# Early tiles of self-attention: normalising and turning spread over six middle rounds of a cross-attention loop

## What is computed

```python
x = x + _L0_xattn_ref(_layernorm(x), ctx_768, ...)   # 16 heads of 16, keys and values from the context
x = x + _L0_attn_ref(_layernorm(x), ...)             # rmsnorm * norm_w, q/k/v projections, causal attention
x = x + _L0_ffn_ref(...); x = x + _L1_xattn_ref(...); x = x + _L1_attn_ref(...); x = x + _L1_ffn_ref(...)
```

## Time and profile before

| | us |
|---|---|
| three runs | 1916.33, 1922.88, 1923.32 |
| median | 1922.88 |
| profiled execution | 1919.42 |
| its span, first to last instruction | 1917.6 |

### The profile page before, as it was taken

One profiled execution on the slowest core, in us unless ns is written; L12 is line 12 of the kernel. 1 busy time (PEld: TensorE's weight loads), 2 busy tenths in 40 slices (PEclk: granted clock), 3 DMA queues, 4 the chain that ended last, 5 costly groups with the idle time before them and its releaser, 6 DMA issues.

```text
span 1917.6 us, 44031 instructions
## 1 busy us (share of the span) xinstructions
PE 1819.1 (95%) x17698; PEld 1540.1 (80%) x17698; DVE 1275.4 (67%) x2718; ACT 940.7 (49%) x2038; POOL 912.3 (48%) x1133
## 2 busy tenths in 40 slices
PE   5999999999999789999999999999999999899998
PEld 4788888888888667879999999999999976656665
DVE  5788888888888765656666767666666745752222
ACT  4666666666666534453444444444444434522221
POOL 4677777777777427337433333343333213513232
PEclk9999999999999897999999999999999999999999
DMA  5112111211111010042223222222233006051110
GB/s 158 37 44 64 37 37 37 60 48 36 37 36 51 9 46 1 2 113 80 81 76 85 61 61 61 61 61 61 65 86 92 1 29 261 1 187 30 24 32 13
DMA packets 50424, 113.06 MB, mean 59 GB/s; under 512 B 4864, under 2 KB 36944, under 8 KB 48688
## 3 DMA queue, kind: packets, MB, share of 16 engines
q1 hardware_dynamic: 45808, 105.13, 18.5%
q0 software_dynamic: 4416, 5.12, 1.5%
HBM read 105.78 MB, written 5.37 MB: 58 GB/s over the span
## 4 chain that ended last, share of the span: by engine, by line
PE 77%; DVE 9%; ACT 7%; issue 3%; DMA 2%; POOL 0%; SPq 0%; POOLq 0%; DVEq 0%; ACTq 0%
PE ps L164 8%; PE ps L104 7%; PE ps L2578 6%; PE ps L495 5%; PE ps L476 5%; PE ps L1642 4%; PE ps L453 4%; PE ps L2602 3%; PE ps L470 3%; PE ps L1643 2%; DVE arena L1754 2%; PE ps L404 2%; DVE arenaR L1748 2%; PE ps L1629 2%; PE ps L1628 2%
## 5 line engine op out<-in xcount | busy, mean ns | idle before, releaser
L562 DVE TENSOR_REDUCE arena<-ps 128x1 f32<-128x400 f32 (+1 forms) x512 | 257.6, 565 | 92.3 <-PE ps L453 92.2
L700 ACT ACTIVATE arena<-ps 128x384 f32<-128x384 f32 (+1 forms) x512 | 223.5, 525 | 103.5 <-PE ps L476 103.5
L777 POOL TENSOR_TENSOR arena<-arena 128x512 f32<-128x512 f32 (+1 forms) x157 | 204.7, 1304 | 92.6 <-ACT arena L700 82.9
L1642 PE MATMUL ps<-arenaR 128*128 128x386 f32 x768 | 242.9, 374 | 1.1 <-DVE arenaR L1748 1.1
L1858 ACT CAST arenaR<-ps 128x512 fp32r<-128x512 f32 (+1 forms) x256 | 116.6, 508 | 202.2 <-PE ps L164 201.4
L1643 PE MATMUL ps<-arenaR 128*128 128x194 f32 x768 | 194.3, 253 | 0.0
L1748 DVE TENSOR_TENSOR arenaR<-ps,arenaR 128x512 fp32r<-128x512 f32 (+1 forms) x256 | 138.9, 585 | 28.6 <-ACT arenaR L1858 28.6
L1643 PEld LDWEIGHTS ps<-arenaR 128*128 128x128 f32 x768 | 147.5, 192 | 0.0
L1642 PEld LDWEIGHTS ps<-arenaR 128*128 128x128 f32 x768 | 145.5, 189 | 1.4 <-DVE arenaR L1748 1.4
L1883 ACT ACTIVATE wsb<-ps,arena 128x1200 f32<-128x1200 f32 x64 | 80.9, 1264 | 131.6 <-DVE arena L1807 131.6
L1754 DVE TENSOR_REDUCE arena<-ps 128x1 f32<-128x400 f32 (+1 forms) x256 | 137.2, 566 | 1.5 <-PE ps L1632 1.4
(11 more groups left out here) (372 smaller groups left out, 4806.8 us busy)
## 6 DMA issues: line engine op xcount, KB each, us to landing
wsb<-in_ctx SPq DMA_DIRECT2D x16, 1152.0 KB
arena<-in_ctxT SPq DMA_DIRECT2D x16, 800.5 KB, 5.2
arena<-in_ctxT SPq DMA_DIRECT2D x32, 400.2 KB, 7.3
wsb<-in_ctxT SPq DMA_DIRECT2D x16, 800.5 KB, 5.1
wsb<-in_ctxT SPq DMA_DIRECT2D x32, 400.2 KB, 7.4
gu<-in_m_gu SPq DMA_DIRECT2D x8, 1536.0 KB, 18.0
dn<-in_m_dn SPq DMA_DIRECT2D x8, 768.0 KB, 10.3
wsb<-in_f_w SPq DMA_DIRECT2D x2, 1024.0 KB, 6.1
```

What stands on the lines that cost most here:

```text
L562: e.tensor_reduce(mx4[n % 2][:, u, i:i + 1], ps[:, at("look", n, i, u), 0:400 + (i == 3)], AX.X, ALU.max).then_inc(c.maxed.at((n, i, u)), 1)
L700: e.activation(v[:, u, 0:128 * GN[s]], ps[:, at("st", n, s, u), 0:128 * GN[s]], ACT.Exp).then_inc(c.exp_a.at((x0, n, s, u)), 1)
L777: e.tensor_tensor(acc_p[0:k], acc_p[0:k], v[0:k, :, 128 * t:128 * t + 128], ALU.add).then_inc(added_p.at((n, s)), 1)
L1642: e.matmul(o, PTh[:, t, :], v[:, t, 0:386], start=(t == 0), stop=False)
```

## The change

Tiles 0 to 5 (`SA_EARLY = 6`) are normalised one by one at the end of DVE's rounds 51 to 56 and turned one by one at the end of PE's rounds 52 to 57, both halves of a tile in one bank. ACT alone copies them out of PSUM, with `norm_w`, into the plain transposed buffer `hT` (`take_h`, two copies of 128 x 128), in its same round; the buffer is free since the last queries of the first stage. In round 60 ACT copies all six tiles (1536 columns) from `hT` to the high part, and in round 61 DVE subtracts to get the low part; both read SBUF. POOL's roots move to round 50 and cover six tiles. Tiles 6 and 7 are normalised, turned (four transposes) and taken between the projections; ACT takes the high part after its share of tile 0's projection instead of tile 1's, DVE the low part ahead of tile 1's sum of squares instead of behind it. The gammas move to round 0. Of the weight copies on ACT one stays at the end of round 59, one moves into round 60 behind the first exponentials, one to the end of round 61, one stays in 63; the weight subtractions on DVE are in rounds 59, 60, 62 and 63. For the last pair the two accumulators lie in the buffers of the weights `wk` and `wv`, which are no longer read, so its first additions wait for no totals.

```diff
-    acc_d, acc_p = ar(128, 4, 128), ar(128, 4, 128)
+    sums_d, sums_p = ar(128, 4, 128), ar(128, 4, 128)
+    def acc(n):
+        if n < N - 1:
+            return sums_d, sums_p
+        return [flat(W[k]).rearrange("p (u c) -> p u c", c=128) for k in ("wk", "wv")]
...
             if s == 0:
-                if n:
-                    w.wait_ge(*(added_p((n - 1, "all")) if n < N - 1 else totals(n - 1)))
+                if n == N - 1:
+                    w.wait_ge(*w_lo("wk"))
+                elif n:
+                    w.wait_ge(*added_p((n - 1, "all")))
...
             if s == 0:
-                if n:
+                if 1 <= n < N - 1:
                     w.wait_ge(*totals(n - 1))
...
             for use in groups(r)[:1]:
                 exps(*use)
+            then.act(e, w, r, 0, at)
...
-            then.act(e, w, r, at)
+            then.act(e, w, r, 1, at)
...
-SA_PARTS = ((0, 1, 2, 3), (4, 5, 6), (7,))
+SA_EARLY = 6
...
-    return [(r - 60, k) for k in range(2)] if r in (60, 61) else []
+    return r - 52 if 0 <= r - 52 < SA_EARLY else None
...
+    def turn_pe(e, w, t, bank):
+        w.wait_ge(*c.normed((sa, t)))
+        for k in range(2):
+            p = c.turn(e, ps[:, bank, 128 * k:128 * k + 128], c.h[:, t, 128 * k:128 * k + 128])
+        p.then_inc(c.hT_turned.at((sa, t)), 1)
+
+    def turn_last_pe(e, w, k):
+        w.wait_ge(*c.normed((sa, NT - 1)))
+        for i in range(2):
+            p = c.turn(e, ps[:, k, 128 * i:128 * i + 128], c.h[:, SA_EARLY + i, 128 * k:128 * k + 128])
+        p.then_inc(c.hT_turned.at((sa, "last", k)), 1)
...
-    def dve_ahead(e, w, r, at):
-        if r == 59:
+    def dve_ahead(e, w, r):
+        if r == 0:
...
-            for t in SA_PARTS[0]:
-                norm_tile_rms(e, w, t)
-        if r == 60:
-            for t in SA_PARTS[1]:
-                norm_tile_rms(e, w, t)
-        if 60 <= r <= 63:
-            split_low(e, w, r - 60)
-        for part, k in sa_turns(r):
-            take_low(e, w, part, k, at("sa", part, k))
+        if 0 <= r - 51 < SA_EARLY:
+            norm_tile_rms(e, w, r - 51)
+        if r in (59, 60, 62, 63):
+            split_low(e, w, (59, 60, 62, 63).index(r))
+        if r == 61:
+            u = slice(0, 128 * SA_EARLY)
+            w.wait_ge(*c.hT_act((sa, "high")))
+            e.tensor_tensor(hTl[:, :, u], hT[:, :, u], hTh[:, :, u], ALU.subtract).then_inc(c.hT_dve.at((sa, "early")), 1)
...
             if t == 0:
+                norm_tile_rms(e, w, SA_EARLY)
                 norm_tile_rms(e, w, NT - 1)
...
-            squares(t)
             if t == 1:
                 for k in range(2):
-                    take_low(e, w, 2, k, k)
+                    take_low(e, w, k)
+            squares(t)
...
+    def take_h(e, w, t, bank):
+        w.wait_ge(*c.hT_turned((sa, t)))
+        w.wait_ge(*c.q_made(("x0", NT - 1)))
+        w.wait_ge(*c.in_const("small"))
+        w.wait_ge(*c.po("zeros"))
+        for k in range(2):
+            p = e.activation(hT[:, k, 128 * t:128 * t + 128], ps[:, bank, 128 * k:128 * k + 128], ACT.Identity, bias=c.zeros[:, 0:1],
+                             scale=c.normw[:, k:k + 1])
+            p.then_inc(c.hT_act.at((sa, t) if k else None), 1)
...
-        for i in {59: (0, 1), 60: (2,), 63: (3,)}.get(r, ()):
+        for i in {(59, 1): (0,), (60, 0): (1,), (61, 1): (2,), (63, 1): (3,)}.get((r, place), ()):
             split_high(e, w, i)
-        for part, k in sa_turns(r):
-            take_high(e, w, part, k, at("sa", part, k))
+        if place and sa_turns(r) is not None:
+            take_h(e, w, sa_turns(r), at("sa", sa_turns(r)))
+        if (r, place) == (60, 1):
+            u = slice(0, 128 * SA_EARLY)
+            w.wait_ge(*c.hT_act((sa, SA_EARLY - 1)))
+            ctx_done(w)
+            e.copy(hTh[:, :, u], hT[:, :, u]).then_inc(c.hT_act.at((sa, "high")), 1)
...
             project(t)
-            if t == 1:
+            if t == 0:
                 for k in range(2):
-                    take_high(e, w, 2, k, k)
+                    take_high(e, w, k)
...
-        u = slice(NT - 1, NT) if last else slice(0, NT - 1)
+        u = slice(SA_EARLY, NT) if last else slice(0, SA_EARLY)
...
     def pool_ahead(e, w, r):
-        if r == 58:
+        if r == 50:
             root_rms(e, w, False)
```

More of the change, by code:

```diff
@@ L337, in latents @@
             at("o", projects(r))
-        for part, k in then.turns(r):
-            at("sa", part, k)
+        if then.turns(r) is not None:
+            at("sa", then.turns(r))
         if r == 2 * N - 2:
@@ L500, in values @@
                 w.wait_ge(*padded("rows"))
+                acc_d, acc_p = acc(n)
                 for u in range(4):
@@ L542, in pe @@
                 project(projects(r))
-            for part, k in then.turns(r):
-                bk = take("sa", part, k)
-                then.turn_pe(e, w, part, k, bk)
-                emptied[bk] = c.hT_dve(("sa", part, k))
+            if then.turns(r) is not None:
+                bk = take("sa", then.turns(r))
+                then.turn_pe(e, w, then.turns(r), bk)
+                emptied[bk] = c.hT_act(("sa", then.turns(r)))
     def dve(e, w):
@@ L649, in dve @@
                 invert(r // 2 - 1)
-            then.dve(e, w, r, at)
+            then.dve(e, w, r)
         gather(N - 1)
@@ L766, in add @@
         def add(n, s):
-            v = probs(n, s)
+            v, acc_p = probs(n, s), acc(n)[1]
             w.wait_ge(*c.exp_a((x0, n, s, 3)))
             if s == 0:
-                if n:
+                if 1 <= n < N - 1:
                     w.wait_ge(*totals(n - 1))
@@ L781, in add_both @@
             w.wait_ge(*added_p((n, 3)))
-            e.tensor_tensor(acc_p, acc_p, acc_d, ALU.add).then_inc(added_p.at((n, "all")), 1)
+            e.tensor_tensor(sums_p, sums_p, sums_d, ALU.add).then_inc(added_p.at((n, "all")), 1)
         def scale(n):
@@ L840, in latents @@
     return pe, dve, act, pool, sp, ended, raw_done, ctx_done
-SA_PARTS = ((0, 1, 2, 3), (4, 5, 6), (7,))
+SA_EARLY = 6
 def sa_turns(r):
-    return [(r - 60, k) for k in range(2)] if r in (60, 61) else []
+    return r - 52 if 0 <= r - 52 < SA_EARLY else None
 def selfattn(c, m, ahead, ctx_done, ended, then):
-    d, ps, psf = c.d, c.ps, c.psf
+    d, ps, psf, hT = c.d, c.ps, c.psf, c.hT
     parts = Carve(m.sap)
@@ L897, in sp @@
         e.dma_start(caus, d["causal"]).then_inc(in_caus.at("in", 16), 16)
-    def part_of(t):
-        return 0 if t < 4 else 1 if t < NT - 1 else 2
-    def columns(part):
-        return slice(128 * SA_PARTS[part][0], 128 * SA_PARTS[part][-1] + 128)
-    def turned(part, bank):
-        return ps[:, bank, 0:128 * len(SA_PARTS[part])]
     def project_pe(e, w, t, which, emptied):
@@ L913, in project_pe @@
             o = slice(512 * (i % 2), 512 * (i % 2) + 512)
-            w.wait_ge(*c.hT_dve((sa, part_of(t), 1)))
+            w.wait_ge(*c.hT_dve((sa, "early") if t < SA_EARLY else (sa, 1)))
             w.wait_ge(*w_lo(i))
@@ L922, in project_pe @@
         return p
-    def turn_pe(e, w, part, k, bank):
-        w.wait_ge(*c.normed((sa, SA_PARTS[part][-1])))
-        o = turned(part, bank)
-        for i, t in enumerate(SA_PARTS[part]):
-            p = c.turn(e, o[:, 128 * i:128 * i + 128], c.h[:, t, 128 * k:128 * k + 128])
-        p.then_inc(c.hT_turned.at((sa, part, k)), 1)
+    def turn_pe(e, w, t, bank):
[8 more added lines that the diff above has]
+        p.then_inc(c.hT_turned.at((sa, "last", k)), 1)
     def pe_ahead(e, w, emptied):
@@ L1010, in pe @@
             w.wait_ge(*emptied[k])
-            turn_pe(e, w, 2, k, k)
-            emptied[k] = c.hT_dve((sa, 2, k))
+            turn_last_pe(e, w, k)
+            emptied[k] = c.hT_dve((sa, k))
         project(2, (2, 3, 0, 1))
@@ L1036, in norm_tile_rms, with take_low @@
     def norm_tile_rms(e, w, t):
-        w.wait_ge(*c.po(("rooted", sa, t == NT - 1)))
+        w.wait_ge(*c.po(("rooted", sa, t >= SA_EARLY)))
         e.tensor_scalar(c.h[:, t, :], c.x[:, t, :], c.mv[:, t, 0:1], c.rs[:, t:t + 1],
                         ALU.subtract, ALU.mult).then_inc(c.normed.at((sa, t)), 1)
-    def take_low(e, w, part, k, bank):
-        u = columns(part)
-        w.wait_ge(*c.hT_act((sa, part, k)))
-        w.wait_ge(*c.in_const("small"))
-        e.scalar_tensor_tensor(hTl[:, k, u], turned(part, bank), c.normw[:, k:k + 1], hTh[:, k, u], ALU.mult,
-                               ALU.subtract).then_inc(c.hT_dve.at((sa, part, k)), 1)
+    def take_low(e, w, k):
+        u = slice(128 * SA_EARLY, 1024)
+        w.wait_ge(*c.hT_act((sa, "last", k)))
+        e.scalar_tensor_tensor(hTl[:, k, u], ps[:, k, 0:256], c.normw[:, k:k + 1], hTh[:, k, u], ALU.mult,
+                               ALU.subtract).then_inc(c.hT_dve.at((sa, k)), 1)
     def split_low(e, w, i):
```

13 lines of the change are left out of this document (6 added, 7 removed).

## The result

The changed kernel took 1905.65 us (median of 10 runs, 1899.91 to 1913.18) against 1918.96 us (10 runs, 1912.12 to 1925.27) of the kernel before: 0.9933 times, 95% interval 0.9912 to 0.9955. By that ratio it is 12.9 us less (13.3 by the two medians).

The account below looks back on a forecast made before the run. The prediction took TensorE (PE), busy 95% of the span, as the bound, with losses where it waits or runs at low clock. +2.7 - 15.2 - 2.2 - 2.2 = -16.9 us from a mean of 1920.5 gave 1904 us, range 1898 to 1914.

Parts of the forecast that it names:

- Middle rounds: Rounds 51 to 57: two added PE transposes in each of six rounds cost 0.45 us a round, +2.7 us; ends 1.6 and 5.
- gap plus shift are 1.03 us, so the pair is covered: Middle rounds: ScalarE's two new copies, about 0.8 us, fit its 0.58 us gap plus PE's 0.45 us later scores.
- a rest of 0.3 would delay maxima: Middle rounds: DVE's added normalisation is hidden for 1.1 of 1.35 us; the rest delays only maxima whose banks PE needs next round.
- Rounds 59 to 64: Last cross-attention rounds: without L1046's waits and with early last-head additions, the first projection starts 16.0 us earlier, taken as 15.2.
- in this chain no wait of PE is over 1.5 us: Rounds 61 and 62: PE runs from scores to totals, ending near 659.5, with no wait above 1.5 us.
- 0.8 us for operations of DVE and POOL that fall on each other: Last rounds: allowance for DVE and POOL additions colliding, reducing the 16.0 us gain to 15.2.
- second rival: Last rounds: the adders bind, DVE's order keeps its old pace, gain 9 us instead of 15.2, 1910 us; chance 0.13.
- The twelve matmuls: First projections: matmuls now at the low clock, 0.43 us each, would run at 0.23, saving some 11 x 0.20 = 2.2 us.
- first rival: From 655 us on the clock stays low, giving back 4.4 us and the twelve matmuls' 2.2 us, 1910 us; chance 0.15.
- The wait for L1046 in the projections: Projections: PE's 2.5 us wait for DVE's low part goes, less 0.27 us for two more transposes, net 2.2 us.
- The third rival: Nothing comes of it: another bank or POOL's additions replace L1046, only the 2.5 us wait goes, 1920 us; chance 0.06.
- the fourth: Rival: turnings stall PE in rounds 52 to 57 and the clock falls there, making it slower, up to 1955 us; chance 0.04.

Follow-up runs that it names:

- e7: Changed kernel with each early tile turned and copied ahead of the round's value products on PE and ScalarE; 1905.14 us in one execution, rounds 51 to 57 71.81 us.
- e5: Changed kernel with tile 0's normalisation moved behind the queries' copy in DVE's round 52; 1901.75 us in one execution, rounds 51 to 57 71.59 us.
- e4: Changed kernel with the last head's sums back in the common place, waiting for the totals before; 1907.67 us, 0.9934 of the kernel before.
- e9: Changed kernel with POOL's additions for head 30's last two groups cut to a quarter width; round 59 to the first projection 38.58 us against 40.0.
- e6: Changed kernel with DVE's last three weight subtractions moved to rounds 62, 63 and 64; 1911.11 us in one execution, round 59 to projection 38.90 us.
- e3: Kernel before with only the last head's sums in their own place; 1918.97 us, 0.9989 of the kernel before.
- e2: Changed kernel, unchanged, profiled a second time; span 1897.9 us, round 59 to the first projection 40.03 us.

## Why the prediction came out as it did

The total, 1904 against 1905.65 us, came out close, the gain did not: forecast 16.9 us, measured 12.9 to 13.3. That the total is nearer is luck in part, since the forecast started from 1920.5 us and the kernel before measured 1918.96. Of the terms one was right, two were too hopeful and one held only at times. The profile's own difference agreed with the sum of -16.9 us by luck (7.5 us of it in self-attention's scores).

**Middle rounds, +2.7 forecast, +3.7 measured.** The price of the turning on PE was over the mark: 0.22 us a round for two transposes (0.38 us as a group, 0.45 assumed with the switch). What failed is the step "gap plus shift are 1.03 us, so the pair is covered". It asked whether the exponentials would be late, and they were not. But the bank has a second client, PE's fourth look, and that one waits for the end of the copies: 0.28 to 0.29 us in rounds 53, 55 and 57, which e7 gave back, and 0.43 us in round 56, which it did not. Likewise "a rest of 0.3 would delay maxima": the first normalisation delayed the queries' copy instead, 1.0 us once, which e5 gave back. I had followed DVE's list to its next wait and not to the operation that frees a bank. The roots cost nothing, as put. The ends of the range, 1.6 and 5, held the value.

**Rounds 59 to 64, -15.2 forecast, -11.9 measured.** The mechanism was right: both waits for L1046 vanish, the second scores of round 61 start 5.3 us earlier (654.35; 654.8 by the forecast with its 2.7 us), and e4 shows that this comes without the own place for the sums. The size was not. The first step that failed is "in this chain no wait of PE is over 1.5 us": the totals of head 30 waited 3.29 us for DVE's additions and came at 664.4 to 664.8, forecast 662.2. From there all is late. DVE's last two pairs were forecast to begin at 664.2, 666.9 with the 2.7 us, and begin at 670.21, 3.3 us late. The 5.4 us from there to the last addition held: 5.44 us, to 675.65. So "what is late then is DVE's adding" was right, and the mis-sized term is "0.8 us for operations of DVE and POOL that fall on each other". The two pairs of head 30 took 3.44 and 3.45 us beside POOL and take 1.41 alone, 4.1 us over in these two alone; the same pairs took 1.40 and 2.37 us in the kernel before, at 659.28 and 664.04. DVE's list has no gap from 650 us on, so that a collision is paid in full, but one that is taken away comes back in part as another: e9 took 3.5 us off and won 1.4, e6 took a subtraction of 1.47 us away and won 1.1. That is the second rival, the adders, with part of its price: it said 9 us of gain, the forecast 15.2, and it was 11.9. Two smaller things were misread. POOL's last addition was put at 667.5 (670.2 with the 2.7 us) and ended at 673.94. And the operations that leave DVE's list up to 657 us come to about 5 us in the trace of before, not 6.

The Trainium skill ("SBUF — State Buffer", "Who interferes with whom"), quoted in the prediction for the normalisations only, bears on these additions: by it a DVE instruction that reads two SBUF inputs and a GpSimd instruction that reads SBUF contend. The pairs at 1.41 us alone and 3.44 us beside POOL agree. It belonged to the term of the last rounds, where DVE has no slack; in the middle ones it bore once, on the 1.35 us normalisation ahead of the queries' copy.

**The first additions of the last head.** The prediction counted POOL's early start as part of the gain. e3 gives it 3.2 to 3.4 us, in a list of DVE that still has gaps of 2.8 and 3.3 us (waits for exponentials, at 663.51 and 671.97); e4 gives it 0.0 us in the changed kernel. It starts at 660.81, just as DVE's pair at 660.84 does, and the one stretches the other.

**The twelve matmuls, -2.2 forecast.** The premise "the 4.0 us wait ahead of them goes" failed: 2.13 us for POOL and 1.28 us for DVE were left. Behind them the clock was 0.66 and the first projections took 0.63 us (0.43 apart) until 679.3, seven slow ones instead of ten, which is 0.6 us. (The forecast counted eleven; ten would have been 2.0 us.) In e2 the granted clock was 1.00 from 675 to 680 and the stretch of the projections took 47.82 us, 1.3 us less than the profiled run's 49.13. So the term is real when the clock is there, and in nine of the ten profiles with the moved turning (48.9 to 50.0 us) it isn't. The first rival was therefore partly true as well: its 4.4 us assumed the low level from 655 on, and up to 665 the table shows 1.00.

**The wait for L1046 in the projections, -2.2 forecast.** 2.5 us are gone: DVE does this part (L1051) in 0.86 us at 691.43 and PE doesn't wait. Right.

**The third rival and the fourth** are out: the last rounds gave 11.9 us and not nothing, and from 540 to 630 us the granted clock of the changed kernel is 1.00 in spite of the added stalls.

```profile
540.00:630.00 90.00, 88.42 (x1422) 72.29 (x1424) 74.04 (x128) 62.38 (x142) 64.49 (x64) 1.00 0.11 37
```

**The signs of being wrong** that the prediction named came true in part, though its total held. The first projection came at 676.15, forecast 673, inside the bound of 678. Rounds 53 to 57 grew by 0.35 to 0.63 us, 0.50 on average (52.21 against 49.70 us for the five), inside the bound of 0.8; round 52 grew by 1.24 us, outside it. A bank of the looks did wait for the new copies, PE did wait for over 3 us (3.29), and the granted clock was not 1.00 from 640 on. (The rounds of the kernel before take 8.3 to 11.0 us in its trace, not 9.3 to 10.3 as the text on it says.)

## What to carry to other kernels

When a stall of the main engine goes, sum up the whole list of the engine that comes next, from the point where its last gap ends; with no gap left, its operations count at their length beside the other engine, not at their median. A bank that rotates has two clients, the engine that empties it and the next user: ask of a moved or added copy not only whether its own engine is late, but when the next user of that bank asks for it. And two removed waits need not add up: the early start of POOL was worth 3.2 to 3.4 us alone and nothing once DVE was full.

## What the runs showed of the hardware that I had not expected

How much the two vector engines stretch each other on plain fp32 additions of 128x512. A pair takes DVE 1.41 us alone and 3.44 us beside POOL. It takes POOL 2.63 us while DVE has its maxima and other small operations (651.57), and 3.93 us beside DVE's additions (655.90).

That the same program comes back to the full clock in one execution and stays at 0.50 for the 20 us shown in another, so that a stretch of 70 us differs by some 4 or 7.5 us between profiles; a single profile can't price an edit of a few us unless the stretch with the edit is cut out and compared by itself.
